# Attention units of two layers interleaved by a table of beats: side steps moved up to one beat, and one pause beat fewer between the layers

## The reference, cut to what matters

```python
x = x + xattn(layernorm(x), ctx)      # 4 batches, 256 tokens, 128 channels; 16 heads of 8; keys and values from ctx
x = x + ffn(layernorm(x))             # ffn:
    # h = rmsnorm(x); q, k, v = h @ Wq + bq, h @ Wk + bk, h @ Wv + bv     (16 query heads, 4 key heads of 8)
    # q, k = rmsnorm(rope(q)), rmsnorm(rope(k));  causal softmax attention;  out * sigmoid(out @ Wg + bg)
    # x = x + out @ Wo + bo;  h2 = rmsnorm(x);  top-1 of 8 experts;  x + expert(h2)
```

## Time and profile before

| | us |
|---|---|
| three runs | 249.04, 250.34, 246.78 (median 249.04) |
| the profiled execution, whole | 247.82 |
| its span in the profile | 246.0 |
| mean granted TensorE clock | 0.882 of full speed |

### The profile page before, as it was taken

How to read it: one execution, slowest core, us unless ns; L and a number is a source line. 1 busy time by engine, 2 the same in 40 slices (tenths; PEclk the granted TensorE clock), 3 DMA queues, 4 the chain that set the end, 5 groups by cost and what they waited for, 6 DMA issues and landing times.

```text
span 246.0 us, 4688 instructions
## 1 busy us (share of the span) xinstructions
PE 179.4 (73%) x1419; PEld 111.0 (45%) x1430; DVE 153.9 (63%) x400; ACT 120.6 (49%) x267; POOL 130.0 (53%) x236
## 2 busy tenths in 40 slices
PE   1783877988796795985985798795884520799991
PEld 0552543545453443642542454453332320688881
DVE  1674778777888884778598578778215252255651
ACT  3344343566554675734553566364371132276660
POOL 8577559153135536657678956526138432036454
PEclk9999955899999999999799799999597555599997
DMA  5476667622485345348147135164211201443000
GB/s 167 130 164 196 183 163 201 190 82 64 135 223 179 111 124 182 96 122 259 38 116 238 55 81 150 49 195 174 118 54 43 88 0 48 123 127 106 27 28 0
DMA packets 22037, 29.69 MB, mean 121 GB/s; under 512 B 3807, under 2 KB 17163, under 8 KB 21143
## 3 DMA queue, kind: packets, MB, share of 16 engines
q1 hardware_dynamic: 19968, 26.72, 37.1%
q0 software_dynamic: 960, 1.59, 2.0%
q10 hardware_dynamic: 1084, 1.09, 1.7%
HBM read 14.73 MB, written 14.98 MB: 121 GB/s over the span
## 4 chain that ended last, share of the span: by engine, by line
PE 43%; DVE 22%; issue 10%; DMA 9%; POOL 9%; ACT 3%; SPq 1%; POOLq 1%; another core or an unknown queue 0%; DVEq 0%; ACTq 0%
PE S L1265 13%; PE O L1265 11%; PE MXX L1265 9%; DVE NEGM L1000 7%; PE MS L1265 5%; DMA QA<-MTS 3%; DMA QA<-q_rows 3%; PE MS L1516 2%; POOL RQ L700 1%; POOL RT L698 1%; POOL RT L697 1%; DVE MHL L1010 1%; DVE QKVS L1157 1%; DVE HR L1216 1%; DMA rooms<-HR,PLACE 1%
## 5 line engine op out<-in xcount | busy, mean ns | idle before, releaser
L1000 DVE TENSOR_REDUCE NEGM<-MXX 128x2 f32<-128x512 f32 (+1 forms) x112 | 74.6, 686 | 23.2 <-PE MXX L1265 20.2
L904 ACT ACTIVATE EX<-S 128x512 f32<-128x512 f32 x112 | 61.2, 594 | 34.5 <-PE S L1265 34.3
L1265 PE MATMUL MXX<-KA,QA 96*128 96x256 bf16 (+1 forms) x256 | 47.5, 284 | 10.2 <-DVE NEGM L1000 5.2
L1265 PE MATMUL S<-QA,KA 128*128 128x256 bf16 (+1 forms) x172 | 37.7, 324 | 2.0 <-DMA QA<-MTS 1.7
L1265 PEld LDWEIGHTS MXX<-KA,QA 96*128 96x128 bf16 x256 | 21.7, 105 | 30.9 <-DVE NEGM L1000 13.7
L690 POOL TENSOR_SCALAR_AFFINE_SELECT EX<-EX 128x512 f32<-128x512 f32 x32 | 20.1, 640 | 14.8 <-ACT EX L904 14.8
L1265 PE MATMUL O<-EX,VB 128*32 128x256 f32 (+1 forms) x256 | 18.0, 355 | 7.0 <-POOL EX L690 5.2
L1265 PE MATMUL O<-EX,VA 128*32 128x256 f32 x256 | 20.9, 399 | 2.2 <-issue 1.9
L1265 PEld LDWEIGHTS S<-QA,KA 128*128 128x128 bf16 x176 | 17.4, 103 | 10.6 <-ACT EX L904 3.6
L763 POOL DMA_INDIRECT out<-KA x8 | 7.9, 984 | 18.4 <-DVE KA L1086 15.9
L1265 PE MATMUL S<-HJ,VA 128*128 128x128 f32 x120 | 17.6, 294 | 0.0
(11 more groups left out here) (196 smaller groups left out, 326.6 us busy)
## 6 DMA issues: line engine op xcount, KB each, us to landing
rooms<-FILL SPq DMA_DIRECT2D x8, 1028.0 KB, 6.0
QA<-q_rows SPq DMA_DIRECT2D x24, 192.0 KB
k_rows<-PT SPq DMA_DIRECT2D x12, 192.0 KB, 3.3
W<-in_w SPq DMA_DIRECT2D x8, 258.0 KB, 5.7
KA<-k_rows SPq DMA_DIRECT2D x9, 192.0 KB
q_rows<-PT SPq DMA_DIRECT2D x24, 64.0 KB, 2.8
KA<-rooms SPq DMA_DIRECT2D x8, 128.5 KB, 2.0
W<-in_w SPq DMA_DIRECT2D x8, 128.0 KB, 5.3
```

Source lines behind the costliest of these rows:

```text
L904: act.activation(EX[g % PRING][:, 512 * half:512 * half + 512], S[n % SRING], ACT.Exp)\
L1000: dve.tensor_reduce(out=NEGM[:, q, heads[0]:heads[-1] + 1], in_=MX[g % 2][:, 0:len(heads) * w].rearrange("p (h t) -> p h t", t=w), axis=AX ...
L1265: return nc.tensor.matmul(out_, lhsT, rhs, start=start, stop=stop, **kw)
```

## The change

The pause goes from 2 beats to 1, so unit 4 and all behind it have places one beat earlier. The steps of the chain move: `o_t` and `on` by 0.25, `on_t` and `ont` by 0.5, `pj` to `ht` by 0.75, `qkv` to `qn` by one beat, `qn_t` to `part3` by 0.75. `z` stays, and so do `o_sb` and all of `AT2`. No instruction is added or taken away, and SyncE's order is the same.

```diff
-        PAUSE = 2
+        PAUSE = 1
...
-        AT1 = {"pj": 19.5, "x1": 19.75, "rstd2": 20.75, "hz_t": 21.25, "ht": 21.5, "qkv": 22.25, "qkvs": 22.5,
-               "squares": 22.75, "ssq": 24, "newton": 24.25, "qn": 26.25, "qn_t": 26.75, "qkf": 27, "rest1": 27.75,
-               "part2": 28.5, "part3": 29, "z": 35}
+        AT1 = {"pj": 18.75, "x1": 19, "rstd2": 20, "hz_t": 20.5, "ht": 20.75, "qkv": 21.25, "qkvs": 21.5,
+               "squares": 21.75, "ssq": 23, "newton": 23.25, "qn": 25.25, "qn_t": 26, "qkf": 26.25, "rest1": 27,
+               "part2": 27.75, "part3": 28.25, "z": 35}
...
-        BOTH = {"o_sb": 17, "o_t": 17.5, "on": 17.75, "on_t": 18.5, "ont": 18.75}
+        BOTH = {"o_sb": 17, "o_t": 17.25, "on": 17.5, "on_t": 18, "ont": 18.25}
```

## The result

The change makes the kernel slower: 257.87 us median of four runs (257.33 to 262.95), beside 248.3 for the kernel before on the same chip; the ratio is 1.0456, 95% interval 1.0392 to 1.052. Forecast were 251.8 and a range up to 255.2, so the sign was right and the size was not. The profiled execution took 257.33 us (span 255.6), 9.5 more than that of before.

What follows compares the result with a forecast made beforehand. No engine was full over the span; VectorE and TensorE hand each other work, so only waits could change. Terms 0.4 + 1.8 - 0.75 + 0.4 + 0.2 + 0 + 1.4 gave +3.4 us; forecast 251.8, between 251.2 and 252.4, range 246.2 to 255.2.

Steps and rivals of the forecast that it cites:

- SSQ at VectorE: Sign in the trace: the sum SSQ standing in front of MHL on VectorE would show the steps right.
- the transposes ending units 2 and 3: Sign: transposes of line 1462 later than 73.14 and 92.43 by about 1 show steps right; old times or earlier, wrong.
- The pause term, +0.2: Layer boundary: filling TensorE's two waits does not shorten them; bounds -2.4 and +0.7, taken +0.2 us, nothing won.
- The third mask of unit 5: GpSimd in unit 5: the mask delayed behind Z and ZB to 144.8, its O 1.3 us late.
- `o_t` in unit 1: Unit 1: same wait for the copy, but a bank and its maxima come behind it; 0 to 0.7, taken +0.4 us.
- The stacks' loads: Units 6 and 7: stacks land 2 to 3 us later, costed at nothing; waits there would show them underpriced.
- unit 4's term: Unit 4: filling the QN wait gives -0.6 to -1.2 us, offset by the third mask's O 0.6 late; taken 0.
- The x1 block, -0.75: A bank now between VectorE's `x1` block and MHL shortens TensorE's wait in unit 2; 0 to -1.12, taken -0.75 us.
- from unit 6 on: 0: From unit 6 on: the second layer's chain keeps its places relative to its unit, Z in idle GpSimd time; 0.
- The sum and guess in front of MHL, +1.8: Units 2 and 3: SSQ and guess on VectorE delay MHL; bounds 0 and 1.33 each, taken 0.9 each, +1.8 us.
- Behind QN on ScalarE, +0.4: ScalarE: ONT, QKF and PT stand in front of exponentials, so scores wait; 0 to 1.57, taken +0.4 us.
- Z, 0 in unit 4 and +1.4 in unit 5: Z and ZB before the third mask on GpSimd: unit 4 0.6 late, regained; unit 5 +1.4 out of 0 to 2.5 us.

Runs made afterwards that it cites:

- g2: The changed kernel with `o_t` to `ont` and `pj` to `squares` back at their old places and `z` one beat earlier: 251.98 us, ratio 1.0149 to the kernel before.
- h1: The kernel before, pause still 2 beats, with only `o_t` to `ont` and `pj` to `ht` at their new places: 256.77 us, ratio 1.0425.
- g4: The changed kernel with `x1` to `squares` back at their old places and `z` one beat earlier: 259.64 us, ratio 1.0458 to the kernel before.

## Why the prediction was wrong

**What held.** Most rows that were to show the steps right are there. SSQ at VectorE stands in front of MHL, and the transposes ending units 2 and 3 are late, at 74.78 and 95.87. The pause term, +0.2: the pause alone measured 0.9975 (0.9911 to 1.004), so nothing that can be seen is won by it. The third mask of unit 5: it starts at 149.50 with the unit's transpose 4.7 us late, which is 144.8 on the old scale, as worked out, and its O waits 0.88 for it. `o_t` in unit 1: that half is 10.0 us instead of 9.6 with `o_t` alone moved. The stacks' loads cost nothing (0.2 us in front of one bank). And the waits as a whole: my sum was +3.4, and TensorE's idle time grew by 4.4. That is in part luck, since the terms below err in both directions.

**The step that failed first: a wait was priced at its length.** Each term of the sum is a duration that lies on the path. But in the two traces 5.6 of the 10.0 us are the same instructions taking longer, with more of them at 1.2 instead of 2.4 GHz, which no term had. I had read the clock of two stretches and a transpose that takes 0.45 instead of 0.30, and in unit 4's term I used it for a possible gain; that waits added to full stretches could bring more of the same I did not price. The kernels with fills show it: with idle time filled with useless work the change is 1.9% instead of 4.6% over the kernel before, and the kernel before gets 1.9% faster. How much of it is the clock where the fills stand is known less well: in the profiled executions 3.5 of 5.9 us and 2.4 of 2.7 us lie there. The Trainium skill has it on the page "TensorE: Matmul & The Clock Gate", in the part on the clock gate, that the clock follows how busy TensorE has recently been; the windows at 75.85 and 76.83 agree, 0.98 us idle and then 0.55 of the clock. In unit 4, where I had hoped that a filled wait would help, it did not: the wait for QN went from 2.02 to 1.19 us, and the granted clock is 0.52 from 120.9 to 124.4, as it was from 116.3 to 119.7 before.

**The x1 block, -0.75, has the wrong sign.** I took that a bank between the block and MHL frees MHL. It does (2.7 us of waits become 0.9), but the banks then wait themselves, 1.39 in the first unit, and 5.3 us in all instead of 2.8; and by the clock it became the dearest single move where it was measured apart from the rest of the chain (1.0425 against 1.0141).

**`o_t` was counted once.** The step moves in all eight units; I priced unit 1. Up to the sixteenth transpose it waits for the copy in five of them (3.9 us), and `on_t` for ON in five (2.6), against the 2.5 of O that they replace. In the same way **"from unit 6 on: 0"** is wrong: these stretches grew by 1.5 and 1.4, with `o_t` waiting 1.29 at 183.34.

**The sum and guess in front of MHL, +1.8.** In the change the two halves grew by 0.2 and 0.7, so 0.9 together; in g2, where the x1 block is late, by 1.3 and 1.4. The mechanism is right, the size depends on its neighbours, and as the term I thought largest it was not the carrier.

**Behind QN on ScalarE, +0.4.** The wait is there and was sized low: scores wait for exponentials, which stand behind ONT, QKF and PT, 0.53 us at 83.53 and 0.64 at 103.88, where the kernel before has no such wait.

**Z, 0 in unit 4 and +1.4 in unit 5.** Measured 1.9% together. I had followed the mask to the product that reads it, and let the fill of `qn_t` pay for it. Beside Z, at 126.30, the two XN took 0.50 us, against 0.48 in h1 at 62.60, where GpSimd began a small SM at 62.77; beside a mask QN's second part took 0.65 us at 119.02, and 0.22 at 78.13. So the rule of the Trainium skill ("SBUF — State Buffer", on the two physically separate sides), by which Z beside the x1 block would add up to Z's length, shows in the second pair and not in the first; whether XN ran in a mode to which the rule applies, no row tells.

What stays open: how the x1 block, Z and the second half share the 4.6% in the whole change. Put back in different company, the x1 block gave 2.8%, and the block together with Z gave nothing (g4). What decides whether a stretch at half clock comes is open too. If it is what else waits nearby, no fixed share exists; that is argued, not shown.

## What to carry to other kernels

Where TensorE is nearly full, price a new wait on it twice: at its length, and at the stretch of half clock that may follow, here 3.6 us of work at 1.6 to 1.7 times its time (`o_t` 1.09 instead of 0.66 us, O 1.08 instead of 0.64). Before moving a step, list every copy of it in the program and what stands directly behind it on its engine; a table that was good at one spot is often the balance of several such waits, and moved either way it loses. And where waits can't be removed, try idle matmuls in them: 69 of them took 1.9% off the kernel before.

## What was not expected of the hardware

TensorE fell to 1.2 GHz after waits of only about 1 us among full work (0.69 and 0.97 within 3 us, at 74.0 and 76.8), stayed there for most of 3.57 us of unbroken work, and went back. A wait of 1.00 us in the same place of the kernel before, with waits of 0.53 and 0.97 around it at 71.7 and 79.5, left it at 2.4 GHz. Useless matmuls that made TensorE busy for 192.0 us instead of 184.4 made the changed kernel over 5 us faster.
